# First attention of a two-layer block: probabilities transposed by DMA, and each item's work spread over six steps

## The chip, the cores and the metric

One NeuronCore of a Trainium2 chip. The metric is device time in microseconds (us) from start to end of the program: before the change 837.07 (median of 3 runs, 836.23 to 838.88).

## What is computed

A "macaron" block of two layers on 4 x 256 tokens of width 256: half a feed-forward net, attention, half a feed-forward net, twice, each behind a layer norm. The change is in the first attention (16 query heads and 4 key heads of 128, rotary embedding, softmax over a banded mask):

```
q = q * cos + _rotate_half(q) * sin
k = k * cos + _rotate_half(k) * sin
...
scores = jnp.einsum('bhqd,bhkd->bhqk', q, k) * scale
mask = iq >= ik - WIN
scores = jnp.where(mask[None, None, :, :], scores, -inf)
attn = jax.nn.softmax(scores, axis=-1)
out = jnp.einsum('bhqk,bhkd->bhqd', attn, v)
return out.transpose(0, 2, 1, 3).reshape(b, s, H * DH) @ Wo.T
```

The second layer's feed-forward net is a mixture of 8 experts, which routes rows of tokens through tables in DRAM (`xs_rows`, `yt_rows`).

## The kernel before, in words

Every product runs with operands split into two f16 parts, a high part (ScalarE copies it) and a low part (VectorE subtracts the high part), in three passes (`product`). The order of the work is written out by hand: each engine has its own list, and the lists meet only in semaphores.

The attention goes over two halves of the tokens (`hf`, two sequences of 256 each). In a half there are 32 items, one per head and sequence, and a step of `step0(hf, p, x)` starts one: `p` counts pairs of heads (8), `x` the four items of a pair. `x` 0 and 1 belong to one head, 2 and 3 to the next. The helper `lagged(p, x, k, n)` names the item started k steps ago. An item's life before the change:

- TensorE (L1672 to L1713): scores into a PSUM bank (step 0), four f32 transposes of the probabilities (L1695, two steps later), values times probabilities (three steps later), projection with Wo (four steps later).
- VectorE, DVE in the profile (L1252 to L1282): maximum of each row (L1258), shift (L1261), low half of the transposed probabilities (L1274), reciprocal of the sums (L1278), low half of the output (L1281).
- ScalarE, ACT in the profile (L744 to L772): high half of the transposed probabilities (L751), two exponentials (L757), high half of the output (L763).
- GpSimd, POOL in the profile (L597 to L609): scales the probabilities by the reciprocals (L607).

Between these stands the rope of the next heads, one head per two steps: TensorE's query product into bank `QB` (`queries`, at `x` 0 and 2), two ScalarE copies that swap halves (`rope_swapped`, L737, L738, at odd `x`), on VectorE the cosine product out of PSUM (`rope_cosine`, L1244, at even `x`), on GpSimd the sine product (`rope_sine`, L590, at odd `x`) and the sum (`rope_add`, L595, at even `x`), then the high half on ScalarE (`rope_high`, L742) and the low half on VectorE (`rope_low`, L1250). A query product waits until the cosine of the head before has read the one bank:

```
if x in ((1, 2) if isinstance(p, int) and p == 0 else (0, 2)) and ...:
    queries(hf, 2 * p + 2 + x // 2, QB, r + 2 + x // 2, r + 2 + x // 2)
```

The steps `p` = 1 to 6 are a loop on every engine. The items still in the pipe at the end of the first half are finished among the key, value and first query products of the second half, those of the second half in the first step of the feed-forward net that follows (`last_steps0`). The output is added to X on DVE (L1012).

SP issues the DMAs: all loads at the start, then twice a zero fill (L469) and a column of "free" marks (L471) for the two tables `xs_rows`, one per expert pass; it then has nothing to do until the attention's last projection.

Of the kernel before, what the change touches and what calls it, by code (L numbers as in the profile page):

```python
# [88 lines left out]
def macaron(nc, x_in, wa_in, wb_in, wc_in, wd_in, wg_in, rope0_in, rope1_in, mask_in, idf_in,  # L89
# [3 lines left out]
    with ctx:  # L93
# [46 lines left out]
        PR0 = ARENA[:, 0:1024].rearrange("p (a n) -> p a n", a=2)  # L140
        PT0 = ARENA[:, 1024:2048].bitcast(F16).rearrange("p (a s n) -> p a s n", a=2, s=2)
# [27 lines left out]
        IDP = sb("IDP", [P, ROWS // P + TT], I32)  # L169
        FREE = sb("FREE", [P, ROWS // P], F32)  # L170
# [19 lines left out]
        XS = [nc.dram_tensor(f"xs_rows{m}", [ROWS, ROW], F32, kind="Internal").ap() for m in range(2)]  # L190
# [20 lines left out]
        QB, OB = 4, 7  # L211
# [35 lines left out]
        pt_done, pt_hi, pt_lo = sem("pt_done"), sem("pt_hi"), sem("pt_lo")  # L247
# [167 lines left out]
        def lagged(i, x, k, n):  # L415

            if isinstance(i, int) and not 0 <= 4 * i + x - k < 4 * n:
                return None
            return (i - 1 if x < k else i), (x - k) % 4
# [27 lines left out]
        def _(sp):  # L447
# [19 lines left out]
            for table in XS:  # L467
                t3 = table.rearrange("(a p) d -> p a d", p=P)
                sp.dma_start(t3[:, :, 0:D + 1], ROUT[:, 0:D + 1].rearrange("p (o n) -> p o n", o=1)  # L469
                             .broadcast_to([P, ROWS // P, D + 1])).then_inc(dma_z, 16)  # L470
                sp.dma_start(t3[:, :, D + 1:ROW], FREE[:, :].rearrange("p (a o) -> p a o", o=1),  # L471
                             allow_slow_non_contiguous=True).then_inc(dma_z, 16)
            sp.wait_ge(proj_done, 2 * NS0)
# [6 lines left out]
            def expert_blocks(m):  # L480
# [3 lines left out]
                for b in range(NBK):  # L484
# [4 lines left out]
                    sp.dma_start(XB[:, g % 3, :], XS[m][ds(row * P, P), :]).then_inc(xb_in[g % 3], 16)  # L489
# [6 lines left out]
            expert_blocks(0)  # L496
            expert_blocks(1)
# [7 lines left out]
        def _(pool):  # L505
# [44 lines left out]
            def scatter(n, hf, tiles=range(TPH)):  # L550

                m = ROUTED.index((n, hf)) // 2
                pool.wait_ge(dma_z, 64)
                pool.wait_ge(idx_done, ROUTED.index((n, hf)) + 1)
                for t in (TPH * hf + i for i in tiles):
                    for k in range(2):
                        pl.indirect_dma_start(XS[m], bass.IndirectOffsetOnAxis(ap=IDX[:, k, t:t + 1], axis=0),  # L557
# [39 lines left out]
            def step0(hf, p, x):  # L597
                st, r = NS0 * hf + 4 * p + x, RU * hf + KV0 + 2 * p
                more, before = not (isinstance(p, int) and p == P0 - 1), not (isinstance(p, int) and p == 0)
# [4 lines left out]
                pool.wait_ge(recip_done, st + 1)  # L604
                pr = PR0[:, x % 2, :].rearrange("p (q k) -> p q k", q=2)
                rs = ST[:, x % 2, 3, :].rearrange("p (q k) -> p q k", k=1)
                pl.tensor_tensor(pr, pr, rs.broadcast_to([P, 2, S]), ALU.mult).then_inc(norm_done, 1)  # L607
# [42 lines left out]
            attention0(1, 2, 0)  # L650
            run_glu(pool, 1, 0, glu_step, glu_side)
# [28 lines left out]
        def _(act):  # L680
# [63 lines left out]
            def step0(hf, p, x):  # L744
                st, r = NS0 * hf + 4 * p + x, RU * hf + KV0 + 2 * p
                more, before = not (isinstance(p, int) and p >= P0 - 1), not (isinstance(p, int) and p in (0, P0))
                if lagged(p, x, 2, P0):
                    act.wait_ge(pt_done, st - 1)
                    after(act, pv_done, st - 3)
                    bank = odd_bank(hf) + 1 if x % 2 else 6  # L750
                    sc.activation(PT0[:, x % 2, 0, :], PS[:, bank, :], ACT.Copy, scale=SP).then_inc(pt_hi, 1)  # L751
                if lagged(p, x, 0, P0):

                    act.wait_ge(shift_done, st + 1)
                    bank = odd_bank(hf) if x % 2 else 5
# [18 lines left out]
            def attention0(hf, n, th):  # L774
# [16 lines left out]
                if hf:  # L791
                    value_high(0)
# [1246 lines left out]
```

## Time and profile before the change

| | |
|---|---|
| runs (3), median | 837.07 us |
| the profiled execution, own time | 835.15 us |
| its span, first to last instruction | 833.3 us |
| mean granted TensorE clock | 0.936 |
| busy over the span: PE, DVE, ACT, POOL | 86%, 75%, 55%, 48% |
| busy in the stretch 180 to 200 us (inside the attention): PE, DVE, ACT, POOL | 19.74, 15.81, 16.07, 13.62 of 20 us |
| first scores of the first half, of the second half | 110.5, 239.9 us |
| last projection of the attention | 351.8 us |

Busy time is the time in which an engine had an instruction under way. Matmuls are pipelined, so that the starts of two that follow each other are nearer together than the durations say: how fast TensorE streams is read from starts, how long an engine is held likewise. An idle time stands in brackets behind a row, with the engine and line that ended it. Times within the span are from its start.

### The profile page before, as it was taken

The numbers are of one execution on the slowest core, as the hardware profiler recorded it, in microseconds if no ns is written. First come the engines' busy times: TensorE is split into PE (matmuls) and PEld (weight loads), VectorE is DVE, ScalarE is ACT, GpSimd is POOL, SyncE is SP. The second block draws the span as 40 slices with busy tenths as digits, with TensorE's granted clock in tenths as the row PEclk, the third lists the DMA queues.
The fourth block names the chain that finished last, engine by engine and source line by source line (L and its number), as shares of the span: only waits on it lengthen the run. The fifth ranks groups of instructions, "written<-read, shape, count | busy, mean of one in ns | idle before, by whom it ended". The sixth has DMA issues, their size and how long they took to land. (4 is left out here: it accounts for less than half of the span.)

```text
span 833.3 us, 17601 instructions
## 1 busy us (share of the span) xinstructions
PE 712.8 (86%) x5515; PEld 481.6 (58%) x5515; DVE 627.9 (75%) x1436; ACT 458.0 (55%) x1033; POOL 402.5 (48%) x412
## 2 busy tenths in 40 slices
PE   7898969999969999989898699765698498978985
PEld 3555447777637777655555466433586397645652
DVE  5989878778787878699977677544897687676656
ACT  3444568878758888545423266325474476324551
POOL 4544766667667667358636177324004320331440
PEclk9999979999999999999999799966799598998998
DMA  9999995000000000030001233300000010012324
GB/s 375 327 300 185 226 231 2 0 0 0 2 0 1 0 0 0 6 116 1 1 14 58 77 114 110 129 1 1 1 1 2 7 46 2 1 52 84 116 84 164
DMA packets 64945, 59.07 MB, mean 71 GB/s; under 512 B 29106, under 2 KB 59186, under 8 KB 64370
## 3 DMA queue, kind: packets, MB, share of 16 engines
q1 hardware_dynamic: 60706, 47.85, 23.7%
q0 software_dynamic: 3744, 10.26, 3.5%
q8 instruction: 36, 0.59, 0.3%
q14 instruction: 27, 0.22, 0.1%
q10 hardware_dynamic: 432, 0.15, 0.1%
HBM read 27.92 MB, written 30.33 MB: 70 GB/s over the span
## 5 line engine op out<-in xcount | busy, mean ns | idle before, releaser
L1492 PE MATMUL PS<-XT,WA 128*128 128x512 f16 x432 | 100.4, 380 | 0.0
L607 POOL TENSOR_TENSOR ARENA<-ARENA,ST 128x512 f32<-128x512 f32 x64 | 66.6, 1040 | 64.0 <-DVE ST L1278 64.0
L724 ACT ACTIVATE ARENA<-T 128x512 f16<-128x512 f32 (+1 forms) x56 | 35.2, 628 | 109.9 <-DVE T L1156 102.4
L1492 PE MATMUL PS<-WA,ARENA 128*128 128x256 f16 (+2 forms) x960 | 68.6, 212 | 12.9 <-DVE ARENA L1165 11.9
L1492 PEld LDWEIGHTS PS<-WA,ARENA 128*128 128x128 f16 x960 | 56.6, 97 | 29.4 <-DVE ARENA L1165 18.0
L566 POOL DMA_INDIRECT yt_rows<-WA,DIX x46 | 45.4, 987 | 55.4 <-ACT WA L856 43.4
L1492 PEld LDWEIGHTS PS<-XT,WA 128*128 128x128 f16 (+1 forms) x432 | 42.3, 98 | 44.1 <-issue 0.8
L1492 PE MATMUL PS<-KVR,ARENA 128*128 (+1 forms) x384 | 57.9, 279 | 7.9 <-DVE ARENA L1250 4.6
L1258 DVE TENSOR_REDUCE ST<-PS 128x2 f32<-128x512 f32 x64 | 43.9, 686 | 26.1 <-PE PS L1492 25.3
L757 ACT ACTIVATE ARENA<-PS,ST 128x256 f32<-128x256 f32 x128 | 59.3, 470 | 7.0 <-DVE ST L1261 6.8
L1492 PE MATMUL PS<-XT,WC 128*128 128x512 f16 x264 | 60.6, 379 | 2.4 <-DVE T L1149 1.4
L595 POOL TENSOR_TENSOR T<-T 128x512 f32<-128x512 f32 x40 | 52.6, 1314 | 8.1 <-DVE T L1244 2.6
L590 POOL TENSOR_TENSOR T<-T,ROPE 128x512 f32<-128x512 f32 x40 | 50.9, 1272 | 10.4 <-ACT T L738 10.3
L1492 PE MATMUL PS<-ARENA,KVR 128*128 128x256 f16 x384 | 52.4, 272 | 2.6 <-DVE ARENA L1281 2.5
L1165 DVE TENSOR_TENSOR ARENA<-T,ARENA 128x512 f16<-128x512 f32 (+1 forms) x48 | 42.0, 876 | 16.5 <-ACT ARENA L724 15.9
L1492 PE MATMUL PS<-XT,WB 128*128 128x512 f16 x192 | 48.0, 388 | 5.7 <-DVE T L1244 4.2
L1492 PE MATMUL PS<-WB,ARENA 128*128 (+1 forms) x384 | 52.4, 273 | 0.3 <-DVE ARENA L1281 0.3
L1149 DVE SCALAR_TENSOR_TENSOR T<-T,PS 128x512 f32<-128x512 f32 (+1 forms) x56 | 38.0, 679 | 18.0 <-ACT T L716 17.6
L716 ACT ACTIVATE T<-PS 128x512 f32<-128x512 f32 (+1 forms) x56 | 33.1, 591 | 31.9 <-PE PS L1492 31.7
L1492 PE MATMUL PS<-WE,WA 128*128 x276 | 50.2, 319 | 0.0
L1492 PEld LDWEIGHTS PS<-KVR,ARENA 128*128 128x128 f16 x384 | 32.9, 99 | 26.6 <-issue 7.2
L557 POOL DMA_INDIRECT xs_rows<-XN,IDX x32 | 32.8, 1024 | 32.1 <-DVE IDX L1107 23.6
(184 smaller groups left out, 1803.0 us busy)
## 6 DMA issues: line engine op xcount, KB each, us to landing
xs_rows<-ROUT SPq DMA_DIRECT2D x2, 9252.0 KB, 46.1
WA<-xs_rows SPq DMA_DIRECT2D x46, 129.0 KB
WB<-wb_dram SPq DMA_DIRECT2D x1, 4096.0 KB, 21.4
WC<-wc_dram SPq DMA_DIRECT2D x1, 2304.0 KB, 26.5
WA<-wa_dram SPq DMA_DIRECT2D x4, 512.0 KB, 6.8
WA<-wa_dram SPq DMA_DIRECT2D x1, 2048.0 KB, 12.7
WA<-yt_rows SPq DMA_DIRECT2D x4, 512.0 KB, 4.1
WB<-yt_rows SPq DMA_DIRECT2D x4, 512.0 KB, 5.8
```

The costliest lines, as they stand in the source:

```text
L557: pl.indirect_dma_start(XS[m], bass.IndirectOffsetOnAxis(ap=IDX[:, k, t:t + 1], axis=0), XN[:, t // 2, t % 2, :], None, bounds_check=ROWS ...
L566: pl.indirect_dma_start(YT, bass.IndirectOffsetOnAxis(ap=DIX[:, b:b + 1], axis=0), YB[:, g % 3, :], None, bounds_check=2 * ROWS + 2 * TOK ...
L590: pl.tensor_tensor(t2, t2, ROPE0[:, 1:2, :].broadcast_to([P, 2, S]), ALU.mult).then_inc(rope_sin, 1)
L595: pl.tensor_tensor(T1[:, a, :], T1[:, a, :], T2[:, a, :], ALU.add).then_inc(rope_sum, 1)
L607: pl.tensor_tensor(pr, pr, rs.broadcast_to([P, 2, S]), ALU.mult).then_inc(norm_done, 1)
L716: sc.activation(T1[r, 0, :], PS[r, GATE[a], :], ACT.Tanh, scale=0.5 / (SX * SW)).then_inc(tanh_done, 1)
L724: sc.activation(HH[r, a, 0, :], T3[r, :], ACT.Copy).then_inc(hid_hi, 1)
L757: sc.activation(PR0[:, x % 2, qt * S:(qt + 1) * S], PS[:, bank, qt * S:(qt + 1) * S], ACT.Exp, bias=ST[:, x % 2, 1, qt:qt + 1], scale=SC0 ...
L1149: v.scalar_tensor_tensor(T2[r, 0, :], T1[r, 0, :], 1.0, PS[r, GATE[a], :], ALU.add, ALU.mult).then_inc(gated, 1)
L1165: v.tensor_tensor(HH[r, a, 1, :], T3[r, :], HH[r, a, 0, :], ALU.subtract).then_inc(hid_lo, 1)
L1258: v.tensor_reduce(ST[:, x % 2, 0, :], PS[:, bank, :].rearrange("p (q k) -> p q k", q=2), AX.X, ALU.max).then_inc(max_done, 1)
L1492: ins = te.matmul(dst, left(a), right(b), start=first and n == 0, stop=last and n == 2, skip_group_check=True)
```

## The change

The probabilities are no longer transposed by TensorE. ScalarE and VectorE split them, before transposing, into f16 halves side by side (`PH0`, four buffers), and SP issues one DMA per item that transposes the eight 128 x 128 blocks into `PT0` (four buffers); TensorE waits for its landing (`pt_in`). An item's work now spans six steps: exponentials one step behind the maximum, reciprocal and scaling two, halves of the probabilities three, values five, projection six. The low half of the probabilities now reads SBUF in both inputs. The freed PSUM banks hold a second query bank (`query_bank`) and a second output bank; a query product waits for the cosine one head further back. The two DRAM tables of rows become one, filled once; its column of marks is written again by SP between the two expert passes (`free_rows`), and waits on `dma_z` count accordingly.

```
-                if lagged(p, x, 2, P0):
-                    pe.wait_ge(norm_done, st - 1)
-                    after(pe, pt_lo, st - 3)
-                    bank = odd_bank(hf) + 1 if a else 6
-                    for qt in range(2):
-                        for kt in range(2):
-                            ins = te.transpose(PS[:, bank, kt * S + qt * P:kt * S + (qt + 1) * P],
-                                               PR0[:, a, qt * S + kt * P:qt * S + (kt + 1) * P], IDF[:, :])
-                    ins.then_inc(pt_done, 1)
-                if item := lagged(p, x, 3, P0):
+                if item := lagged(p, x, 5, P0):
                     pp, xx = item
                     g = pp // (GRP // 2)
-                    pe.wait_ge(pt_lo, st - 2)
-                    after(pe, ot_lo, st - 3)
+                    pe.wait_ge(pt_in[xx], turned_count(hf, pp))
+                    after(pe, ot_lo, st - 6)
...
-                    queries(hf, 2 * p + 2 + x // 2, QB, r + 2 + x // 2, r + 2 + x // 2)
+                    queries(hf, 2 * p + 2 + x // 2, query_bank(hf, x // 2), r + 2 + x // 2, r + 1 + x // 2)
```

SP:

```
+            def probabilities(hf, p, x):
+                it = NS0 * hf + 4 * p + x
+                sp.wait_ge(ph_lo, it + 1)
+                after(sp, pv_done, it - 3)
+                sp.dma_start(PT0[x].rearrange("p s (g n) -> p (s g) n", n=P), PH0[x].rearrange("p s n -> p (s n)"),
+                             transpose=True).then_inc(pt_in[x], 16)
...
             expert_blocks(0)
+            free_rows()
             expert_blocks(1)
```

ScalarE:

```
+                if item := lagged(p, x, 3, P0):
+                    pp, xx = item
+                    act.wait_ge(norm_done, st - 2)
+                    after(act, pt_in[xx], turned_count(hf, pp - 1))
+                    sc.activation(PH0[xx][:, 0, :], PR0[xx], ACT.Copy, scale=SP).then_inc(ph_hi, 1)
+                if item := lagged(p, x, 1, P0):
+                    xx = item[1]
+                    act.wait_ge(shift_done, st)
...
                 if x % 2 and more:
-                    rope_swapped(r + 2 + x // 2, QB, x // 2)
-
+                    rope_swapped(r + 2 + x // 2, query_bank(hf, x // 2), x // 2)
+                if item := lagged(p, x, 5, P0):
+                    a = item[1] % 2
+                    act.wait_ge(pv_done, st - 4)
+                    sc.activation(OT0[:, a, 0, :], PS[:, OB + a, 0:S], ACT.Copy, scale=1 / SP).then_inc(ot_hi, 1)
```

GpSimd, in the step (the order sum, scaling, sine stays) and between the key ropes of the second half:

```
-                pool.wait_ge(recip_done, st + 1)
...
+                if item := lagged(p, x, 2, P0):
+                    xx = item[1]
+                    pool.wait_ge(recip_done, st - 1)
...
                     rope_sine(RU * hf + i, i % 2)
                     rope_add(RU * hf + i, i % 2)
+                    if hf and i < 2:
+                        step0(0, P0, i)
```

VectorE: the step now begins with the reciprocal of the item two steps old, then the rope piece, then the low half of the item three steps old, then maximum and shift, and ends with the low half of the output:

```
+                if item := lagged(p, x, 3, P0):
+                    ph = PH0[item[1]]
+                    dve.wait_ge(ph_hi, st - 2)
+                    v.scalar_tensor_tensor(ph[:, 1, :], PR0[item[1]], SP, ph[:, 0, :], ALU.mult,
+                                           ALU.subtract).then_inc(ph_lo, 1)
```

What this does to the order on two engines. First ScalarE, inside the loop. Before, the step `x` = 1 from the high half of the transposed probabilities (L751) to the two rope copies (L737, L738):

```order
L751 ACTIVATE ARENA<-PS 128x512 [waits pv_done,pt_done]
L754 REGISTER_ALU
L757 ACTIVATE ARENA,ST<-PS,ST 128x256 [waits shift_done]
L757 ACTIVATE ARENA,ST<-PS,ST 128x256
L763 ACTIVATE ARENA<-PS 128x256 [waits pv_done]
L734 REGISTER_ALU
L263 REGISTER_ALU [waits rope_in]
L737 ACTIVATE T2<-PS 64x512 [waits rope_sum]
L738 ACTIVATE T2<-PS 64x512
```

Now, step `x` = 1 from the high half of the probabilities (L783) over the exponentials (L789) and the rope copies (L769, L770) to the high half of the output (L797):

```order
L783 ACTIVATE WB<-ROUT 128x512 [waits pt_in2,norm_done]
L786 REGISTER_ALU
L789 ACTIVATE ARENA,ST<-PS,ST 128x256 [waits shift_done]
L789 ACTIVATE ARENA,ST<-PS,ST 128x256
L766 REGISTER_ALU
L269 REGISTER_ALU [waits rope_in]
L769 ACTIVATE T2<-PS 64x512 [waits rope_sum]
L770 ACTIVATE T2<-PS 64x512
L796 REGISTER_ALU
L797 ACTIVATE ARENA<-PS 128x256 [waits pv_done]
```

The high half waits for GpSimd's scaling (`norm_done`) where it waited for TensorE's transposes (`pt_done`); the output's high half has moved from ahead of the rope copies to behind them.

Second VectorE, where an odd step of the loop ends and the even one after it begins. Before, from the low half of the output (L1281) over maximum (L1258), shift (L1261), cosine (L1244) and the low half of the transposed probabilities (L1274) to the reciprocal (L1278):

```order
L1281 SCALAR_TENSOR_TENSOR ARENA<-PS,ARENA 128x256 [waits ot_hi]
L1256 REGISTER_ALU
L1258 TENSOR_REDUCE ST<-PS 128x2 [waits scores]
L1261 TENSOR_SCALAR ST<-ST 128x2 [waits max_done]
L1242 ISA
L1244 TENSOR_TENSOR T1<-PS,ROPE0 128x512 [waits rope_lo,rope_swap]
L1274 SCALAR_TENSOR_TENSOR ARENA<-PS,ARENA 128x512 [waits pt_hi]
L1277 ISA
L1278 RECIPROCAL ST<-ST 128x2 [waits exp_done]
```

Now, from the low half of the output (L1318) over reciprocal (L1293), cosine (L1279), low half of the probabilities (L1305), maximum (L1310) to the shift (L1313):

```order
L1318 SCALAR_TENSOR_TENSOR ARENA<-PS,ARENA 128x256 [waits ot_hi]
L1292 ISA
L1293 RECIPROCAL ST<-ST 128x2 [waits exp_done]
L1277 ISA
L1279 TENSOR_TENSOR T1<-PS,ROPE0 128x512 [waits rope_lo,rope_swap]
L1305 SCALAR_TENSOR_TENSOR WB<-ROUT,WB 128x512 [waits ph_hi]
L1308 REGISTER_ALU
L1310 TENSOR_REDUCE ST<-PS 128x2 [waits scores]
L1313 TENSOR_SCALAR ST<-ST 128x2 [waits max_done]
L1318 SCALAR_TENSOR_TENSOR ARENA<-PS,ARENA 128x256 [waits ot_hi]
```

The cosine has come ahead of maximum and shift, right behind the low half of the output and the reciprocal; the low half of the probabilities reads ROUT (or ARENA) where it read PS.

## Rows read from the trace of the kernel before

**Rows 1.** PE's timeline, 193.5 to 202.8 us: start us, us, engine, line, operation, what ended an idle time.
```profile
193.91 0.49 PE L1492 MATMUL PS<-KVR,ARENA 128*128 x3
...
194.62 0.60 PE L1695 MATMUL PS<-IDF,ARENA 128*128 128x128 f32 x4
195.06 0.82 PE L1492 MATMUL PS<-ARENA,KVR 128*128 128x256 f16 x6
195.71 0.82 PE L1492 MATMUL PS<-WB,ARENA 128*128 x6
...
199.16 1.47 PE L1492 MATMUL PS<-XT,WB 128*128 128x512 f16 x6
200.47 0.49 PE L1492 MATMUL PS<-KVR,ARENA 128*128 x3
```

**Rows 2.** DVE's timeline, the same stretch.
```profile
194.82 0.69 DVE L1258 TENSOR_REDUCE ST<-PS 128x2 f32<-128x512 f32 x1 [1.04 <-PE PS L1492]
...
196.85 0.15 DVE L1278 RECIPROCAL ST<-ST 128x2 f32<-128x2 f32 x1
197.08 0.42 DVE L1281 SCALAR_TENSOR_TENSOR ARENA<-PS,ARENA 128x256 f16<-128x256 f32 x1
197.42 0.68 DVE L1258 TENSOR_REDUCE ST<-PS 128x2 f32<-128x512 f32 x1
...
198.31 0.69 DVE L1244 TENSOR_TENSOR T<-PS,ROPE 128x512 f32<-128x512 f32 x1
198.93 0.69 DVE L1274 SCALAR_TENSOR_TENSOR ARENA<-PS,ARENA 128x512 f16<-128x512 f32 x1
```

**Rows 3.** Timelines of POOL (first four rows) and ACT, 160 to 202.8 us.
```profile
161.03 1.04 POOL L607 TENSOR_TENSOR ARENA<-ARENA,ST 128x512 f32<-128x512 f32 x1
...
198.35 1.27 POOL L590 TENSOR_TENSOR T<-T,ROPE 128x512 f32<-128x512 f32 x1 [0.23 <-ACT T L738]
199.77 1.26 POOL L595 TENSOR_TENSOR T<-T 128x512 f32<-128x512 f32 x1
200.99 1.04 POOL L607 TENSOR_TENSOR ARENA<-ARENA,ST 128x512 f32<-128x512 f32 x1
...
197.07 0.60 ACT L737 ACTIVATE T<-PS 64x512 f32<-64x512 f32 x1
...
198.30 0.60 ACT L751 ACTIVATE ARENA<-PS 128x512 f16<-128x512 f32 x1
...
199.69 0.39 ACT L763 ACTIVATE ARENA<-PS 128x256 f16<-128x256 f32 x1
```

**Rows 4.** Timelines of POOL and DVE at two places, and line L974's durations (min/median/max).
```profile
220.30 1.27 POOL L590 TENSOR_TENSOR T<-T,ROPE 128x512 f32<-128x512 f32 x1 [0.36 <-ACT T L738]
221.72 1.52 POOL L595 TENSOR_TENSOR T<-T 128x512 f32<-128x512 f32 x1
...
220.91 1.21 DVE L1250 TENSOR_TENSOR KVR<-T,KVR 128x512 f16<-128x512 f32 x1
...
336.50 0.89 DVE L1261 TENSOR_SCALAR ST<-ST 128x2 f32<-128x2 f32 x1
...
L974 DVE SCALAR_TENSOR_TENSOR WA<-WA x8: 678/912/1578, 10.4 to 42.0; 128x512 f16<-128x512 f32 x8
```

**Rows 5.** DMA issues: line, engine, operation, count, KB each, median us to landing.
```profile
out_dram<-X SPq DMA_DIRECT2D x4, 256.0 KB, 2.2
...
xs_rows<-FREE SPq DMA_DIRECT2D x2, 36.0 KB, 48.6
```

**Rows 6.** Stretch 220 to 240: its length, busy us by engine, granted clock, DMA share, GB/s.
```profile
220.00:240.00 20.00, 15.04 (x84) 7.89 (x83) 17.62 (x32) 13.23 (x24) 15.20 (x14) 1.00 0.00 1
```

**Rows 7.** Timelines: SP and POOL late in the program, DVE between the halves.
```profile
533.56 0.97 SPq L493 DMA_DIRECT2D WB<-yt_rows  x2
...
664.53 1.08 POOL L557 DMA_INDIRECT xs_rows<-XN,IDX  x1 [10.83 <-DVE IDX L1107]
...
229.03 0.68 DVE L1012 SCALAR_TENSOR_TENSOR X<-PS,X 128x512 f32<-128x512 f32 x1
```

More of the change, by code:

```diff
@@ L598, in step0 @@
                 st, r = NS0 * hf + 4 * p + x, RU * hf + KV0 + 2 * p
-                more, before = not (isinstance(p, int) and p == P0 - 1), not (isinstance(p, int) and p == 0)
+                more, before = not (isinstance(p, int) and p >= P0 - 1), not (isinstance(p, int) and p in (0, P0))
                 if x == 0 and before:
@@ L650, in _ @@
             attention0(1, 2, 0)
+            for x in range(2):
+                step0(1, P0, x)
             run_glu(pool, 1, 0, glu_step, glu_side)
@@ L745, in step0 @@
                 st, r = NS0 * hf + 4 * p + x, RU * hf + KV0 + 2 * p
-                more, before = not (isinstance(p, int) and p >= P0 - 1), not (isinstance(p, int) and p in (0, P0))
-                if lagged(p, x, 2, P0):
[L748 to L755, printed above, removed]
-                    for qt in range(2):
-                        sc.activation(PR0[:, x % 2, qt * S:(qt + 1) * S], PS[:, bank, qt * S:(qt + 1) * S],
-                                      ACT.Exp, bias=ST[:, x % 2, 1, qt:qt + 1], scale=SC0 / SQ ** 2,
-                                      accum_out=ST[:, x % 2, 2, qt:qt + 1]).then_inc(exp_done, 1)
@@ L803, in attention0 @@
                     step0(hf, 0, x)
-                with act.Fori(1, P0 - 1) as p:
+                for x in range(4):
+                    step0(hf, 1, x)
+                with act.Fori(2, P0 - 1) as p:
                     for x in range(4):
@@ L948, in _ @@
             attention0(1, 2, 0)
-            for x in range(3):
+            for x in range(4):
                 step0(1, P0, x)
+            step0(1, P0 + 1, 0)
             act.wait_ge(dma_c, 16)
@@ L1253, in step0 @@
                 st, r = NS0 * hf + 4 * p + x, RU * hf + KV0 + 2 * p
-                more, before = not (isinstance(p, int) and p >= P0 - 1), not (isinstance(p, int) and p in (0, P0))
+                more, before = not (isinstance(p, int) and p >= P0 - 1), not (isinstance(p, int) and p in (0, P0, P0 + 1))
+                if item := lagged(p, x, 2, P0):
+                    a = item[1] % 2
+                    dve.wait_ge(exp_done, 2 * st - 2)
+                    v.reciprocal(ST[:, a, 3, :], ST[:, a, 2, :]).then_inc(recip_done, 1)
+                if x == 0 and before:
+                    rope_cosine(r + 1, query_bank(hf, 1), 1)
+                if x == 2 and more:
+                    rope_cosine(r + 2, query_bank(hf, 0), 0)
+                if x == 1 and before:
+                    rope_low(r + 1, 1, QT0[:, 1, 1, :], QT0[:, 1, 0, :])
+                if x == 3 and more:
+                    rope_low(r + 2, 0, QT0[:, 0, 1, :], QT0[:, 0, 0, :])
+                if item := lagged(p, x, 3, P0):
[3 more added lines that the diff above has]
+                                           ALU.subtract).then_inc(ph_lo, 1)
                 if lagged(p, x, 0, P0):
@@ L1320, in attention0 @@
                     step0(hf, 0, x)
-                with dve.Fori(1, P0 - 1) as p:
+                for x in range(4):
+                    step0(hf, 1, x)
+                with dve.Fori(2, P0 - 1) as p:
                     for x in range(4):
@@ L1465, in _ @@
             attention0(1, 2, 0)
-            for x in range(3):
+            for x in range(4):
                 step0(1, P0, x)
+            step0(1, P0 + 1, 0)
             glu(1, 0)
@@ L1745, in attention0 @@
                 queries(hf, 0, QB, r + KV0, r + KV0 - 1)
-                for i in range(0 if hf else KV0 - 1, TPH - 1):
+                if hf:
+                    step0(0, P0 + 1, 0)
+                    values(0)
+                    step0(0, P0 + 1, 1)
+                for i in range(1 if hf else KV0 - 1, TPH - 1):
                     values(i)
@@ L1758, in attention0 @@
                     step0(hf, 0, x)
-                with pe.Fori(1, P0 - 1) as p:
+                for x in range(4):
+                    step0(hf, 1, x)
+                with pe.Fori(2, P0 - 1) as p:
                     for x in range(4):
```

103 lines of the change are left out of this document (53 added, 50 removed).

## The prediction

> **What bounds the kernel now.** I read four views in turn. The table of stretches first: in the first attention TensorE looks full (19.7 of each 20 us in the table above), so removing its transposes seems to promise their time. The timeline of PE shows what they are. A step (one item's scores and the older items' work) streams scores in 0.71 us, four transposes in 0.44, probabilities times values in 0.65, the projection in 0.65, and every second step a query product of 1.31 [rows 1]. A pair of steps streams 2 x 2.45 + 1.31 = 6.21 us. The period of a pair, over six of them, is (200.99 - 161.03) / 6 = 6.66 us [rows 3]. So 0.45 us of a pair is not TensorE's.
>
> The timeline of DVE says whose it is. DVE idles once per pair, 1.04 us, until the scores behind a query are there, and then works without a gap: reduction, shift, low half of a head, low half of the probabilities, reciprocal, low half of the output, reduction, and at 198.31 the cosine of the next head [rows 2]. That cosine ends at 199.00 and the next query starts at 199.16 [rows 1, 2], because the query waits for the one bank that the cosine reads. Query, scores, seven DVE instructions, cosine, query: this ring has no slack, and it, not TensorE's stream, sets 6.66 us. The change opens it: queries get a second bank and wait for the cosine before. Without it and without transposes PE would need 2 x 2.01 + 1.31 = 5.33 us a pair. What is late next decides everything.
>
> **The ring that the change closes.** Take an odd step of ScalarE (the first order listing) and count from the start of its two rope copies, using today's durations.
> 1. The copies start at 0 and take 1.23 us; the copy of the output now stands behind them and takes 0.39 (198.30 - 197.07, and the row at 199.69) [rows 3]. Done: 1.62.
> 2. DVE (second order listing): the output's low half starts at 1.65, occupies DVE 0.34, the reciprocal 0.23, then the cosine starts at 2.22 [rows 2]. Its sum on POOL could start at 2.22 + 0.69 + 0.08 = 2.99; the sine alone would have let it start at 198.35 - 197.07 + 1.42 = 2.70 [rows 3].
> 3. But 0.62 after the cosine's start DVE issues the new low half of the probabilities, with both inputs in SBUF; the old one read PSUM. Such an instruction and POOL's exclude each other: DVE's subtraction at 220.91 took 1.21 us in place of 0.69, ending 0.55 after POOL's of 220.30 ended, and POOL's next took 1.52 in place of 1.26, ending 1.12 after DVE's [rows 3, 4]. The same form as the new one took 0.68 us at best and 1.58 at worst [rows 4]. Thus: low half 2.84 to 3.52, sum ends 3.52 + 1.12 = 4.64.
> 4. POOL now scales an item two steps old, in the next even step right behind this sum: it ends at about 4.64 + 1.04 = 5.68 (today 1.22 from start to start [rows 3]). I add 0.04 for the shift, which slips in between.
> 5. ScalarE's next odd step begins with the high half of just that item: start 5.76. High half and two exponentials hold it 199.69 - 198.30 = 1.39 today [rows 3]; I take 1.44, since the source is SBUF now, and the next rope copies start at 7.20.
>
> So a pair takes 7.20 us, 0.54 more than now, with PE idle for 1.9 us of it. Without the exclusion of step 3 the chain gives 6.75; without DVE's part as well (sum at 2.70) 6.46. Below that DVE stands: 6.66 less its 1.04 us of idle time is 5.6 us a pair [rows 2, 3]. There are 14 pairs with queries in each half of the tokens, so 28: **28 x 0.54 = +15.1 us**, bounds 28 x (6.46 - 6.66) = -5.6 and, if a second exclusion bites, the rival below.
>
> **Step by step, the rest.**
> - *64 x 4 transposes off PE*: 64 x 0.44 = 28.2 us of stream, worth nothing while the ring holds; in the last eight steps, which have no query, at best 2 x 6 x 0.44 = 5 us. I take nothing, since the shift then also meets POOL's scaling: the shift at 336.50 took 0.89 us, not 0.17, waiting for POOL's instruction [rows 4].
> - *64 DMA transposes of 256 KB on SP's queue*. No row shows one. Lower bound: 256 KB to DRAM landed in 2.2 us. Upper bound: the column of 9216 pieces landed in 48.6 us, 5.3 ns a piece; 1024 rows of 256 bytes would be 5.4 us [rows 5]. I take 3.5, nearer the first, since these are no 4-byte pieces. Between the low half (3.52) and the output's copy two ScalarE steps on, PE has 6 us for it, so both bounds hide as latency. As a rate, transfers must follow each other within 7.2 / 2 = 3.6 us; the upper bound breaks that (rival).
> - The Trainium skill, "DMA: Bandwidth & Descriptors", Latency and other measured facts, gives 261 GB/s for a DMA transpose, an estimate of 1.0 us here, and would leave the sum as it is; "VectorE: DVE Perf Modes", The three transpose paths, gives 1309 ns for one 128x128 block, and taken eight times would be 10.5 us an item. No run here shows either yet.
> - *Deeper pipe, between the halves*. On POOL the last two items' scalings move behind the first and the second rope of the next half. The second sum ends at 223.24 [rows 4]; with two scalings before it or behind, the last item is scaled at about 225.4, its halves take 0.60 + 0.68, the DMA 3.5, the product 0.65, the output's halves 0.9, the projection 0.65: 232.5. DVE adds that result to X at 229.03 today [rows 7]. **+4 us**, and 1 more for the exclusions: **+5**, bounds 1 (the DMA hides) and 9.
> - *At the end of the second half*: flush of six steps in place of four, DMA in place of transposes and a ScalarE copy: 3.5 - 1.0 less cover: **+2**, bounds 0 and 4.
> - *One DRAM table in place of two*: 9.25 MB less to fill, and its column written again between the expert passes. SP issues that behind the gathers at 533.56, and POOL's first scatter of the second pass stands at 664.53 [rows 7]; 48.6 us of landing hide in 131. Nothing. If SP were late, that scatter is what would wait. SP's queue is otherwise idle in the attention.
> - *TensorE's clock*: the stretch 220 to 240 shows 15.04 us busy of 20 at a granted 1.00 [rows 6], and the new loop is as busy (5.33 / 7.2 = 74%). No term.
>
> Sum: 15.1 + 5 + 2 = +22.1 us on the profiled execution's 835.15, so 857.3. The median of the runs is 1.9 above that execution, so I predict **859 us**.
>
> **Rivals.**
> - *Longer ring (slower still)*. Counting on, the shift of an odd step becomes ready 0.1 to 0.2 us before POOL starts the next sine. If it misses, it waits out the 1.27 us [rows 3], and the output's low half with it: the pair takes about 8.2 us, 28 x 1.0 more, 887 us. For it: the margin is smaller than my errors. Against: the rows, added, just miss it.
> - *The DMA rate becomes the bound*. Over 3.6 us per transfer, each 1 us costs 64 us; at 5.4 the kernel takes 859 + 64 x 1.8 = 974. Both the waits for the transfers on PE and SP would show it. Against: the 2.2 us for the same bytes.
> - *Faster: the ring does not close*. If the scaling on POOL ran ahead of the rope sum by an item, so that ScalarE's high half waits for nothing, DVE's and ScalarE's own work would set about 5.5 us a pair: 28 x (5.5 - 6.66) = -32, plus 7 for the flushes: about 812. It decides from the point where a pair falls below 6.5 us. Against: POOL's order is sine, sum, scaling, and ScalarE's wait counts exactly the scaling behind that sum.
> - *Sizes only*: the chain at 6.46, the flushes hidden: 835.
>
> **How the numbers follow.** Forecast 0.50; longer ring 0.20; DMA rate 0.12; faster 0.11; the no-change case 0.07. A measurement of this kernel tells about 0.3% (2.5 us) from no change. Slower: 0.50 + 0.20 + 0.12 = 0.82; same 0.07; faster 0.11. The range reaches down to 840 (the chain without the exclusion at 6.75 is 28 x 0.09 + 5 = +7, less 4 for flushes that hide) and up to 893 (the longer ring with the upper flush bound); left out are the faster case and most of the DMA case. The forecast's own range is 846 to 872.
>
> **What would show it.** Right: no transposes on PE and PE busy near 75%; between two rope copies of ScalarE 7.2 us; ScalarE's high half, now of the probabilities, waits for POOL's scaling; low halves on DVE of over 1 us beside POOL. Wrong: PE waiting for the DMA in each step, SP issuing without a pause, or pairs under 6.5 us with ScalarE or DVE full.

## The result, and the profile after

Four runs of the changed kernel have a median of 854.32 us (850.85 to 855.35), four of the kernel before 837.98 us (836.23 to 840.58). The ratio is 1.019, with a 95% interval of 1.016 to 1.023: 16 us slower. The prediction was 859 us, 840 to 893. The profiled execution took 855.31 us, its span 853.5 us at a mean granted clock of 0.932.

The page of the profile after: busy us and share by engine, and the DMA engines' busy tenths in 40 slices.

```profile
PE 691.6 (81%) x5259; PEld 454.7 (53%) x5259; DVE 651.7 (76%) x1436; ACT 460.1 (54%) x1033; POOL 426.1 (50%) x412
...
DMA  9999114333413334440001233290000010012324
```

PE is busy 691.6 us instead of 712.8, so the transposes did leave it, and the DMA slices 8 to 17, all 0 before, now show the transfers. Inside the attention the same stretch as in the table above (its length, then PE, PEld, DVE, ACT, POOL, the clock, the DMA share, GB/s):

```profile
180.00:200.00 20.00, 16.46 (x129) 11.79 (x129) 16.92 (x36) 14.65 (x41) 14.76 (x12) 1.00 0.40 76
```

PE fell from 19.74 to 16.46 us of 20, DVE and POOL rose from 15.81 to 16.92 and from 13.62 to 14.76. The clock stayed at 1.00. Now one pair of steps in full. ACT's timeline: the two rope copies (L769, L770) start a pair; L797 is the output's high half, L774 the rope's, L783 that of the probabilities, L789 an exponential.

```profile
179.74 0.59 ACT L769 ACTIVATE T<-PS 64x512 f32<-64x512 f32 x1
...
180.97 0.39 ACT L797 ACTIVATE ARENA<-PS 128x256 f16<-128x256 f32 x1
...
184.47 0.63 ACT L774 ACTIVATE ARENA<-T 128x512 f16<-128x512 f32 x1 [1.40 <-POOL T L621]
185.46 0.63 ACT L783 ACTIVATE WB<-ROUT 128x512 f16<-128x512 f32 x1 [0.37 <-POOL ROUT L635]
...
187.03 0.59 ACT L769 ACTIVATE T<-PS 64x512 f32<-64x512 f32 x1
```

From 179.74 to 187.03 is one pair, 7.29 us. ACT waits in it twice for POOL: 1.40 us for the rope sum, 0.37 for the scaling. Over nine pairs (136.64 to 201.44, same row) the period is 7.20 us, by turns 7.13 and 7.30; before it was 6.66. DVE and POOL in the same pair, the rows that answer to [rows 2] and [rows 3]:

```profile
181.39 0.42 DVE L1318 SCALAR_TENSOR_TENSOR ARENA<-PS,ARENA 128x256 f16<-128x256 f32 x1 [0.53 <-ACT ARENA L797]
...
182.02 0.69 DVE L1279 TENSOR_TENSOR T<-PS,ROPE 128x512 f32<-128x512 f32 x1
182.63 0.68 DVE L1305 SCALAR_TENSOR_TENSOR WA<-ARENA,WA 128x512 f16<-128x512 f32 x1
...
183.95 0.51 DVE L1313 TENSOR_SCALAR ST<-ST 128x2 f32<-128x2 f32 x1
```

```profile
181.03 1.27 POOL L616 TENSOR_TENSOR T<-T,ROPE 128x512 f32<-128x512 f32 x1 [1.52 <-ACT T L770]
182.79 1.64 POOL L621 TENSOR_TENSOR T<-T 128x512 f32<-128x512 f32 x1 [0.50 <-DVE T L1279]
184.40 2.48 POOL L635 TENSOR_TENSOR ROUT<-ROUT,ST 128x512 f32<-128x512 f32 x2
```

DVE: output's low half, cosine, low half of the probabilities (182.63), shift (183.95); reciprocal and maximum lie between. POOL: sine (L616), sum (L621), two scalings (L635). The sum takes 1.64 us, where it took 1.26 [rows 3]: it started 0.16 after DVE's low half and got under way behind it. The shift took 0.51 instead of 0.17 and ended with POOL's sum. Over the whole run L1305 has a mean of 1.02 us, where the low half that read PSUM had 0.69.

The transfers: landing, and PE's waits for them (us in total, times, longest).

```profile
ARENA<-WA SPq DMA_TRANSPOSE x32, 3.1
...
PE PS L1532 <- DMA WE<-WB: 2.1, 2, 1.9
...
PE PS L1532 <- DMA WC<-WB: 1.6, 4, 0.6
...
PE PS L1532 <- DMA ARENA<-WA: 1.2, 2, 0.7
```

They land in 3.1 us (median). PE waits for one eight times in the whole run, 4.9 us, and never in the rhythm of the loop: every wait is between the halves or in the last steps.

Where the difference of the two spans, 20.2 us, lies:

| stretch | before | after | difference |
|---|---|---|---|
| first half, first to last scores | 101.4 | 107.3 | +5.9 |
| last scores to first scores of the second half | 28.0 | 31.0 | +3.0 |
| second half, first to last scores | 100.8 | 106.1 | +5.4 |
| last scores to last projection | 11.1 | 13.9 | +2.7 |
| from there to POOL's scatter at 736.74 (before) and 753.82 (after) | | | 0.0 |
| from that scatter to the end | 96.6 | 99.7 | +3.1 |

The last row is no work of the change: in its stretch 817 to 837 the granted clock is 0.91, in the answering stretch of before 1.00. The traced runs of the experiments bear this out: from the same scatter to the end the kernel before takes 99.2 us in e1 and 99.7 in e9 (clock 0.91 there in both), the changed kernel 95.4 us in e3 (1.00). Another run of the changed kernel, at a mean clock of 0.944, has a span of 849.0. So the change itself costs 17.1 us, and the medians say 16.3.

### The profile page after: what moved, and what is told of

Same layout as the page of the kernel before. It is cut to its first block and busy times, and to the rows that moved or that the text cites. A ratio compares the mean times of both kernels' runs of the same rounds, so it can differ in the third digit from the quotient of the medians.

```text
span 853.5 us, 17074 instructions
## 1 busy us (share of the span) xinstructions
PE 691.6 (81%) x5259; PEld 454.7 (53%) x5259; DVE 651.7 (76%) x1436; ACT 460.1 (54%) x1033; POOL 426.1 (50%) x412
## 5 line engine op out<-in xcount | busy, mean ns | idle before, releaser
L616 POOL TENSOR_TENSOR T<-T,ROPE 128x512 f32<-128x512 f32 x40 | 51.7, 1293 | 54.9 <-ACT T L770 54.9
L621 POOL TENSOR_TENSOR T<-T 128x512 f32<-128x512 f32 x40 | 62.8, 1570 | 11.3 <-DVE T L1279 9.2
L1532 PEld LDWEIGHTS PS<-WB,ARENA 128*128 128x128 f16 x384 | 34.9, 98 | 29.5 <-issue 17.5
L1532 PE MATMUL PS<-XT,WB 128*128 128x512 f16 x192 | 50.0, 401 | 0.0
L1532 PE MATMUL PS<-WC,ARENA 128*128 128x256 f16 (+1 forms) x288 | 40.8, 298 | 9.2 <-DVE ARENA L1200 9.1
L925 ACT ACTIVATE ARENA<-PS,LNSP 128x768 f32<-128x768 f32 x32 | 28.9, 902 | 29.4 <-PE PS L1871 29.4
L1310 DVE TENSOR_REDUCE ST<-PS 128x2 f32<-128x512 f32 x64 | 43.6, 681 | 0.0
```

What stands on the lines that cost most here:

```text
L616: pl.tensor_tensor(t2, t2, ROPE0[:, 1:2, :].broadcast_to([P, 2, S]), ALU.mult).then_inc(rope_sin, 1)
L621: pl.tensor_tensor(T1[:, a, :], T1[:, a, :], T2[:, a, :], ALU.add).then_inc(rope_sum, 1)
L925: sc.activation(PR1[:, q % 2, :].rearrange("p (b n) -> p b n", b=2), PS[:, bank:bank + 2, 0:384], ACT.Exp, bias=LNSP[:, :], scale=SC1 / SQ ...
L1310: v.tensor_reduce(ST[:, x % 2, 0, :], PS[:, bank, :].rearrange("p (q k) -> p q k", q=2), AX.X, ALU.max).then_inc(max_done, 1)
L1532: ins = te.matmul(dst, left(a), right(b), start=first and n == 0, stop=last and n == 2, skip_group_check=True)
```

## The experiments

Each ratio is to runs of the kernel before on the same chip, with its 95% interval. "Pair" is the period between the rope copies on ScalarE, read from its timeline in mid-loop.

| run | edit | ratio | pair, us |
|---|---|---|---|
| (the change) | | 1.019 (1.016 to 1.023) | 7.13, 7.30 |
| e1 | before, 1 transpose of 4 | 1.000 (0.998 to 1.002) | 6.56, 6.77 |
| e2 | before, short low half | 0.999 (0.997 to 1.001) | 6.56, 6.77 |
| e3 | after, short low half | 1.007 (1.004 to 1.010) | 6.75, 6.91 |
| e4 | after, transfers twice | 1.023 (1.020 to 1.027) | 7.13, 7.30 |
| e5 | after, scaling before sum | 1.030 (1.026 to 1.034) | 7.35, 7.40 |
| e6 | after, rope's high half late | 1.035 (1.028 to 1.041) | 7.66, 7.80 |
| e7 | after, both | 1.009 (1.006 to 1.012) | 6.86 |
| e8 | after, both, copies first | 1.022 (1.017 to 1.027) | 7.08, 7.47 |
| e9 | before, query late | 0.989 (0.987 to 0.991) | 6.35, 6.40 |
| e10 | before, high half late | 1.119 (1.116 to 1.121) | 10.3, 10.5 |
| e11 | before, both | 1.050 (1.048 to 1.053) | 7.95, 8.16 |
| e12 | e9, 1 transpose of 4 | 0.993 (0.990 to 0.996) | 6.35, 6.40 |

**e1: do the transposes count?** Three of four are left out in the loop steps.

```
-                    for qt in range(2):
-                        for kt in range(2):
+                    whole = isinstance(p, int)
+                    for qt in range(0 if whole else 1, 2):
+                        for kt in range(0 if whole else 1, 2):
```

> The kernel before, with one of the four transposes of an item in the loop steps and the other three left out (their part of the probabilities is stale there). TensorE's stream falls by 3 x 0.11 = 0.33 us in each of 48 steps, 15.8 us in all. My theory: the ring of query, scores, VectorE and cosine bounds a pair at 6.66 us and the transposes lie in its shadow: 0 to -2 us, pairs of 6.6 to 6.66. Rival (TensorE's stream bounds): -14 to -16 us, pairs of 6.0.

837.93 against 838.03 us: nothing. A row of PE's timeline and three of ACT's (an exponential, L757, between two rope copies):

```profile
196.62 0.50 PE L1492 MATMUL PS<-KVR,ARENA 128*128 x3 [0.28 <-DVE ARENA L1250]
...
195.89 0.47 ACT L757 ACTIVATE ARENA<-PS,ST 128x256 f32<-128x256 f32 x1 [0.22 <-DVE ST L1261]
...
197.21 0.59 ACT L737 ACTIVATE T<-PS 64x512 f32<-64x512 f32 x1
...
203.77 0.60 ACT L737 ACTIVATE T<-PS 64x512 f32<-64x512 f32 x1
```

PE now idles (0.28 for the low half of a head, and at 197.79 0.18 for that of the output) where it streamed transposes. ScalarE's exponentials, which stand behind the high half of the transposed probabilities, now wait 0.22 us for VectorE's shift: the shift, not the transposes, lets them start. The pair keeps its 6.56 us, to the digit. So the prize that the change goes for was zero, as predicted.

**e2: is VectorE's queue the ring before?**

```
-    v.scalar_tensor_tensor(PT0[:, x % 2, 1, :], PS[:, bank, :], ...
+    n = 512 if isinstance(p, int) else 64
+    v.scalar_tensor_tensor(PT0[:, x % 2, 1, 0:n], PS[:, bank, 0:n], ...
```

> The kernel before, with the low half of the probabilities on VectorE cut from 512 to 64 columns in the loop steps (the rest is stale there). My theory: one of these stands in the ring between the scores and the cosine, so a pair loses up to 0.5 us until TensorE's stream of 6.21 us ends it: 24 pairs x 0.45 = -9 to -11 us, pairs of 6.2. Rival (TensorE's stream bounds already): under 2 us.

836.92 against 838.03 us, pairs unchanged: a miss. My ring for the kernel before was wrong. Its rows, DVE's between ACT's and PE's:

```profile
192.29 0.59 ACT L737 ACTIVATE T<-PS 64x512 f32<-64x512 f32 x1
...
193.74 0.69 DVE L1244 TENSOR_TENSOR T<-PS,ROPE 128x512 f32<-128x512 f32 x1
194.35 0.21 DVE L1275 SCALAR_TENSOR_TENSOR ARENA<-PS,ARENA 128x64 f16<-128x64 f32 x1
...
194.59 1.47 PE L1493 MATMUL PS<-XT,WB 128*128 128x512 f16 x6
```

The low half (194.35) is short and stands behind the cosine; the one in the other step of the pair is short too, and both only lengthen VectorE's idle time. What then lets the cosine start? In [rows 2, 3] the copies run from 197.07 to 198.28 and the cosine starts at 198.31, and VectorE's own queue ahead of it (output's low half, maximum, shift) ends within 0.03 us of the copies. Both branches start at one instruction, ScalarE's copy of the output at 196.66, so this turn doesn't tell them apart. The other turn of the kernel before does (ACT's second copy, DVE's shift and cosine):

```profile
190.92 0.59 ACT L738 ACTIVATE T<-PS 64x512 f32<-64x512 f32 x1
...
191.53 0.17 DVE L1261 TENSOR_SCALAR ST<-ST 128x2 f32<-128x2 f32 x1
191.75 0.69 DVE L1244 TENSOR_TENSOR T<-PS,ROPE 128x512 f32<-128x512 f32 x1
```

The copies end at 191.51 and the cosine starts at 191.75, behind the shift: here VectorE's maximum and shift, which had to wait for their scores, release it. The cosine comes 1.45 us after the start of the copies (190.30), in the turn of [rows 3] 1.24, and this 0.21 is the difference of the two turns, 6.77 and 6.56 us. So the low half of the probabilities was wrong in my ring, and ScalarE was missing.

Behind the cosine the ring runs on through ScalarE. The rows of the kernel before that close it:

```profile
201.38 0.69 DVE L1258 TENSOR_REDUCE ST<-PS 128x2 f32<-128x512 f32 x1 [0.84 <-PE PS L1492]
202.10 0.17 DVE L1261 TENSOR_SCALAR ST<-ST 128x2 f32<-128x2 f32 x1
...
201.12 0.63 ACT L742 ACTIVATE ARENA<-T 128x512 f16<-128x512 f32 x1 [1.04 <-POOL T L595]
...
202.31 0.47 ACT L757 ACTIVATE ARENA<-PS,ST 128x256 f32<-128x256 f32 x1
...
203.62 0.60 ACT L737 ACTIVATE T<-PS 64x512 f32<-64x512 f32 x1
```

Copies 197.07, cosine 198.31, query 199.16, scores behind it 200.47 [rows 1], maximum 201.38, shift 202.10, exponentials 202.31, output copy 203.22, copies 203.62: 6.55 us. A second ring runs beside it: copies, sine 198.35, sum 199.77, rope's high half 201.12, high half of the probabilities 201.81, the same exponentials. This one has no query and no scores in it. In the kernel before it doesn't bound by itself: the step from 201.12 to 201.81 takes 0.69 us because the high half of the probabilities waits for the transposes (PE 201.18 to 201.78); in e9 the same step takes 0.54.

The total of e2 hides a loss. In its trace one early pair of each half takes 8.14 and 7.88 us instead of 6.45 and 6.46, where the granted clock is 0.50 (120 to 122 and 250 to 252; before 1.00). Of these 3.1 us, 2.7 are made up behind the attention, where nothing was changed.

**e3: does the exclusion cost what the prediction says?** The same cut in the changed kernel, where both inputs are in SBUF.

> The changed kernel, with the low half of the probabilities on VectorE cut from 512 to 64 columns in the loop steps of pairs 2 to 6 (the rest is stale there). My theory: its exclusion with GpSimd's rope sum is 0.45 us of the ring: the sum falls from 1.64 to about 1.3 us and starts no later, pairs go from 7.20 to 6.75 us; 20 pairs x 0.45 = -9 us on the changed kernel's 854, so 845. Rival (the exclusion is beside the path; ScalarE's order behind GpSimd's scaling, or the DMA, sets the pair by itself): under 3 us.

843.49 us, 10.8 less than the changed kernel's median. ACT, DVE and POOL:

```profile
183.60 0.59 ACT L769 ACTIVATE T<-PS 64x512 f32<-64x512 f32 x1
...
190.35 0.59 ACT L769 ACTIVATE T<-PS 64x512 f32<-64x512 f32 x1
...
186.25 0.22 DVE L1306 SCALAR_TENSOR_TENSOR WB<-ROUT,WB 128x64 f16<-128x64 f32 x1
...
186.41 1.26 POOL L621 TENSOR_TENSOR T<-T 128x512 f32<-128x512 f32 x1 [0.26 <-DVE T L1279]
```

The pair is 6.75 us from copies to copies (6.91 in the other turn), the sum back at 1.26. The prediction's chain without the exclusion gave 6.75. The cut makes VectorE's own work shorter too, but the sum waits for the cosine alone (0.26), and the pair fell by 0.38 and 0.39 us, just what the sum lost (1.64 to 1.26): it is the exclusion. It doesn't explain all of the 10.8 us. From the first to the last rope copies of the attention the traces differ by 7.6 us (244.2 and 236.6), which is 20 x 0.38; behind the scatter of the last pass, where nothing was cut, they differ by another 4.3 (99.7 and 95.4).

**e4: is the DMA rate or latency on the path?** Each transpose is followed by a second one of the same size into memory that nobody reads.

```
+                after(sp, dumped, 16 * it)
+                sp.dma_start(DUMP..., PH0[x]..., transpose=True).then_inc(dumped, 16)
```

> The changed kernel, with every DMA transpose followed on the same queue by a second one of the same size into memory that nobody reads, so twice the transfers and bytes. My theory: the transfers' rate and latency are not on the path (each lands in 3.1 us, TensorE has about 6 us for it): 0 to +3 us, and pairs still of 7.2 us. Rival (the DMA rate bounds or is close to it; two transfers of 3.1 us in a step of 3.6): pairs of 12.4 us or, if they overlap by half, over 8 us, +25 us and more.

859.3 us, 5 more than the changed kernel's 854.3 (the ratios, whose intervals overlap, say 4; 0 to 3 were expected), and pairs of 7.13 and 7.30 as before. Landing, and PE's waits:

```profile
WE<-WB SPq DMA_TRANSPOSE x16, 3.3
...
PE PS L1537 <- DMA ARENA<-WA: 4.7, 4, 2.1
...
PE PS L1537 <- DMA WC<-WB: 4.1, 4, 1.7
PE PS L1537 <- DMA WE<-WB: 3.7, 2, 2.0
```

The waits come to 12.5 us where they were 4.9, all between the halves and at the end. In the loop twice the transfers cost nothing.

**e5 to e8: can the new ring be opened?** e5 exchanges two instructions on GpSimd (scaling ahead of the rope sum). e6 moves the rope's high half on ScalarE behind the odd step's exponentials and its low half on VectorE with it. e7 does both; e8 puts the high half behind the rope copies instead, and the low half last in VectorE's step.

```
GpSimd, even steps (e5, e7, e8):  sum, scaling          ->  scaling, sum
ScalarE, odd steps (e6, e7):      exponentials, copies  ->  exponentials, rope_high, copies
VectorE, odd steps (e6, e7):      rope_low ahead of ph_lo  ->  behind the shift
```

> The changed kernel, with GpSimd's scaling of the probabilities ahead of the rope sum in even steps (the prediction's faster rival). My theory now: ScalarE's next step then waits for no scaling, but the sum ends a scaling later (4.9 to 5.5 us after the rope copies' start) and ScalarE's rope high half, which waits for the sum, stands ahead of the next step's work: 0.63 for it, 0.5 for the high half of the probabilities, 1.05 for two exponentials, so 7.1 to 7.75 us a pair, -3 to +15 us on the changed kernel's 854. Rival (the prediction's: ScalarE's wait for the scaling is the whole of it): pairs of 5.5 to 6 us, 812 to 825.

> The changed kernel, with ScalarE's high half of the rope sum moved from the end of an even step to behind the exponentials of the odd one, and VectorE's low half of it behind that step's shift; GpSimd's order as in the change. My theory: the wait for the scaling (5.7 us after the rope copies' start) still stands ahead of the exponentials, and the moved high half adds 0.6 behind them: 7.2 to 7.8 us a pair, 0 to +17 us. Rival (the rope sum itself bounds): pairs of 6.5 or less, under 838.

> The changed kernel with both of these: scaling ahead of the rope sum on GpSimd, and the rope's high half behind the exponentials. My theory: neither wait then stands ahead of the exponentials, and the ring that is left runs rope copies, sine, scaling, sum (ends at 4.9 to 5.5), high half, copies: 5.7 to 6.2 us a pair, 28 x (6.0 - 7.2) = -34 us: 815 to 830, below the kernel before. Rival (VectorE, 5.6 us of work a pair and its waits for GpSimd's port, or PE's waits for the transfers bound first): pairs of 6.6 to 7, 838 to 848.

> As the one with both moves, but the rope's high half stands behind ScalarE's rope copies and output copy of the odd step, and its low half last in VectorE's odd step. My theory: the sum is out of ScalarE's ring altogether, but the scores of the next step and VectorE's next step start only behind the low half (3.0 us after the copies' start): 6.3 to 6.7 us a pair, 829 to 840. Rival (only ScalarE's order counts): 5.6 us a pair, 810 to 815.

863.97, 868.13, 846.87 and 856.0 us. e5 and e6 fell where the chains put them: each takes away one of ScalarE's two waits for GpSimd (1.40 us for the sum, 0.37 for the scaling) and lengthens the other, to 1.93 for the sum in e5 and to 2.40 for the scaling in e6. The prediction's faster rival (pairs under 6.5 once the scaling leads) is refuted by e5. e7, with both, gains 1.0% over the change (the ratios 1.009 and 1.019), but 6.86 us a pair is not 6.0; its rival was right. e8 (7.08 and 7.47, where 6.3 to 6.7 were expected) missed in part for the same reason: its shifts wait for POOL too, and in every second pair one waits out the sine (188.22, 1.27 us instead of 0.17). That is what the prediction's longer ring was to suffer. DVE, POOL and ACT of e7 (L789 is an exponential):

```profile
185.84 1.45 DVE L1301 SCALAR_TENSOR_TENSOR WB<-ROUT,WB 128x512 f16<-128x512 f32 x1
...
187.92 0.52 DVE L1309 TENSOR_SCALAR ST<-ST 128x2 f32<-128x2 f32 x1
...
185.70 1.04 POOL L631 TENSOR_TENSOR ARENA<-ARENA,ST 128x512 f32<-128x512 f32 x1
186.70 1.72 POOL L621 TENSOR_TENSOR T<-T 128x512 f32<-128x512 f32 x1
...
188.48 0.48 ACT L789 ACTIVATE ROUT<-PS,ST 128x256 f32<-128x256 f32 x1 [0.99 <-DVE ST L1309]
```

The low half of the probabilities (L1301) waits for POOL's scaling (1.45 instead of 0.67), the shift (L1309) for POOL's sum (0.52 instead of 0.17), and the exponentials at 188.48 for the shift. The wait that ScalarE no longer has for the sum, it has through VectorE's wait for the same instruction.

**e9 to e12: the kernel before, with what e2 taught.** e9 moves the query product on TensorE from the end of the even step into the odd one, so that the scores no longer queue behind it:

```
+                if x % 2 and not (isinstance(p, int) and p >= P0 - 1):
+                    queries(hf, 2 * p + 2 + x // 2, QB, r + 2 + x // 2, r + 2 + x // 2)
                 if item := lagged(p, x, 3, P0):
...
-                if x in ((1, 2) if isinstance(p, int) and p == 0 else (0, 2)) and not (isinstance(p, int) and p >= P0 - 1):
-                    queries(hf, 2 * p + 2 + x // 2, QB, r + 2 + x // 2, r + 2 + x // 2)
```

> The kernel before, with one edit on TensorE: the query product moves from the end of an even step into the odd one, behind its scores and transposes. My theory after two misses: the ring that bounds the kernel before at 6.66 us a pair runs rope copies (ScalarE), cosine, query, scores behind it on TensorE's queue, reduction, shift, two exponentials, output copy, rope copies; this edit takes the query out from ahead of the scores, and what is left is the ring rope copies, sine, sum, rope high half, high half of the probabilities, exponentials, output copy, 6.45 to 6.55 us: -3 to -6 us. Rival (VectorE's queue between scores and cosine, as the prediction said): no change or, with the query up to 2 us later, slower.

> The kernel before, with the rope's high half moved on ScalarE from the end of an even step to behind the exponentials of the odd one, and its low half on VectorE behind that step's reciprocal. My theory: this opens only the second ring (sine, sum, high half); the one through the query stays at 6.56 and 6.77 us in turn and gets the 0.6 us of the high half between exponentials and copies: 0 to +17 us. Rival (sum and high half bound): faster by 3 us or more.

> The kernel before with both moves. My theory: both rings are open, ScalarE no longer waits for the rope sum, and TensorE's stream of 6.21 us a pair is the next bound: pairs of 6.2 to 6.35 us, 28 x (6.3 - 6.66) = -10 us, 825 to 830, faster than both kernels; the transposes would then be worth their time. Rival (the low half of a head, now late on VectorE, holds up the next even scores): pairs of 6.6 or more, no gain.

e9: 836.36 against 844.16 us on its chip, 1.1% faster than the kernel before, and so faster than both. The pairs, 6.35 and 6.40, are even below what I gave the second ring. ACT, POOL, and the stretch 180 to 200:

```profile
188.34 0.60 ACT L737 ACTIVATE T<-PS 64x512 f32<-64x512 f32 x1
...
192.34 0.63 ACT L742 ACTIVATE ARENA<-T 128x512 f16<-128x512 f32 x1 [0.98 <-POOL T L595]
...
194.69 0.59 ACT L737 ACTIVATE T<-PS 64x512 f32<-64x512 f32 x1
...
191.04 1.27 POOL L595 TENSOR_TENSOR T<-T 128x512 f32<-128x512 f32 x1
...
180.00:200.00 20.00, 19.96 (x167) 16.00 (x165) 18.61 (x38) 16.70 (x48) 14.31 (x13) 1.00 0.00 0
```

ACT works without a pause from 192.34 to the copies at 194.69, and what releases 192.34 is the sum. 28 pairs x (6.66 - 6.37) is 8.1 us; 7.8 were measured. Here too two waits all but coincide: the shift, held up by POOL's scaling (192.45, 0.88 us instead of 0.17), ends at 193.33, and the exponentials start at 193.37.

e10 and e11 are far slower than I expected (945.03 and 888.13 us), and the rival named for e11 came true. In e10:

```profile
188.09 1.31 DVE L1249 TENSOR_TENSOR ARENA<-T,ARENA 128x512 f16<-128x512 f32 x1 [0.35 <-ACT ARENA L742]
...
187.82 1.04 POOL L607 TENSOR_TENSOR ARENA<-ARENA,ST 128x512 f32<-128x512 f32 x1 [3.57 <-DVE ST L1273]
...
189.70 0.55 PE L1491 MATMUL PS<-KVR,ARENA 128*128 x3 [2.39 <-DVE ARENA L1249]
```

The low half of a head, moved late on DVE, meets POOL's scaling, takes 1.31 instead of 0.69 us, and the even scores (PE, 189.70) wait 2.39 us for it; in e11 1.72 us. In e10 the granted clock is low besides, 0.83 in the stretch 180 to 200 where e11 has 1.00; what of its 101 us is the clock's wasn't tried apart. I take it that the move pays only if that low half isn't late; no run shows it, and e11 couldn't show TensorE's 6.21 us.

**e12: with the query's ring open, do the transposes count at last?**

> The kernel before with the query behind the odd scores, and besides with one transpose of the four in the loop steps (three left out, as in the first experiment). My theory: its pairs of 6.35 and 6.40 us are the ring rope copies, sine, sum, rope high half, high half of the probabilities, exponentials, output copy, with no slack on ScalarE; the transposes are not in it: pairs within 0.03 us of these, 0.989 of the kernel before. Rival (with the ring of the query open, TensorE's stream of 6.21 us is what holds a pair at 6.37): pairs of 6.2 or less, 0.984 or less.

838.41 against 844.46 us. PE, and ACT's rope copies:

```profile
189.78 0.52 PE L1492 MATMUL PS<-KVR,ARENA 128*128 x3 [0.40 <-ACT ARENA L757]
...
190.29 0.59 ACT L737 ACTIVATE T<-PS 64x512 f32<-64x512 f32 x1
...
196.64 0.59 ACT L737 ACTIVATE T<-PS 64x512 f32<-64x512 f32 x1
```

PE idles 0.40 us ahead of the scores and 0.27 at 191.06, and in mid-loop the pairs stay at 6.35 and 6.40. The ratio is 0.993 and not 0.989, though the two intervals just overlap. In the trace most of these 3 us is in two pairs of each half, the second and third of the loop: 7.11 and 6.94, and 7.12 and 6.95, where e9 has 6.35 and 6.39, and 6.36 and 6.39. That is 2.6 us. In that place the granted clock of e12 is 0.57 (126 to 130) and 0.60 (252 to 256), that of e9 1.00. So it isn't the rhythm that loses them; that the clock does is my reading of the trace, and no run sets it apart. At any rate nothing is gained.

## Why the prediction was right, and where it was not

- *The transposes are worth nothing*: right, shown by e1, and by e12 even with one ring less.
- *What bounds the kernel before*: the number (6.66 us a pair, a ring through the single query bank) was right, the members were not. The step that failed is the sentence "Query, scores, seven DVE instructions, cosine, query". VectorE's maximum and shift are in it, and then ScalarE's exponentials, output copy and rope copies. The low half of the probabilities is beside it (e2). The next maximum and shift release the cosine in every second pair (191.75) and tie with the rope copies in the others; the other low halves and the reciprocal weren't cut one by one. e9 shows that the query ahead of the scores is in the ring. The step "the change opens it" held, but the ring of ScalarE and GpSimd right behind (6.37 in e9) was missed: even a change that only opened the query's ring had 0.3 us a pair to win.
- *The ring that the change closes*: right in each step that could be read. Copies to output copy 1.23 (predicted 1.23), cosine at 2.28 (2.22), low half at 2.89 (2.84), sum ends at 4.69 (4.64), scaling awaited at 5.72 (5.76), copies at 7.29 (7.20). Part of the last agreement is luck: from the scaling to the copies it is 1.57 us in both turns, where I took 1.44, and the scaling comes at 5.56 in the other turn; in the mean the two errors cancel. The price of the exclusion, 0.45, was 0.38 (e3). The sign "PE busy near 75%" came out as 82% (16.46 of 20 us): the 5.33 us of stream are counted from starts, busy time from durations.
- *The term 28 x 0.54 = 15.1* was 11.3 us (5.9 + 5.4). The difference per pair was right in mid-loop, the count was not: in the first half 12 periods carry it (122.77 to 208.58 after, 123.70 to 203.62 before: +5.9), the steps ahead of the first are 1.1 us shorter and those behind the last 1.1 longer.
- *Between the halves +5*: +3.0. *At the end +2*: +2.7. The DMA took 3.1 us (3.5 taken).
- *DMA*: at twice the rate still not bounding (e4). The landing of 3.1 us lies within the prediction's bounds from rows (2.2 to 5.4) and agrees with neither of the two estimates named behind them, 1.0 and 10.5 us. *One table*: its column was written again at 551.73 and the first scatter that needs it came at 681.22. Nothing, as costed; it wasn't tried apart.
- *TensorE's clock*: no term in the attention, right as to the cost, though the clock isn't 1.00 everywhere: in the first pairs of the loop it falls to 0.50 (124 to 126, and 260 to 262), where before it was 1.00. The pairs there are 6.82 and 7.05 us, the same as in the second half of e3, whose clock is 1.00 there. 3.1 us in the profiled run are from the clock in the last expert pass, a place of which I had said nothing.
- *The rivals*: the longer ring of 8.2 didn't come, though the shift does lose 0.34 us to POOL's sum (183.95): it isn't on the path there, since the exponentials that need it start at 186.00, behind the scaling. In e8 such a wait, of 1.27 us, does come. The faster rival was refuted as a mechanism by e5.

For the profiled execution the sum gave 857.3 us, and it took 855.3. That is closer than the terms deserve: those of the attention were 5.1 us too high (22.1 against 17.0), and 3.1 us of clock in the last pass, which no term foresaw, made up for most of it. That part is luck.

## What to carry to other kernels

An engine that is busy 99% of a stretch need not bound it: leave out part of its work in an experiment, and if its idle time grows by just that, the bound is a ring through other engines' queues. When a wait ends within a few hundredths of two candidates, the trace doesn't say which of them holds; follow each candidate round to where it started, and cut one. And work that moves from a PSUM source to SBUF sources on VectorE should be counted against GpSimd's time too, since the two then run one after the other.

## What the runs showed of the hardware that I had not expected

- The exclusion reaches very small instructions, but not all. A 128x2 multiplication from SBUF to SBUF on VectorE (the shift) took 0.51 us beside POOL's sum and 0.17 without it, and 0.89 in the kernel before at 336.50 [rows 4]; a 64-column low half took 0.83 us beside a scaling and 0.22 alone (e3). The reductions, cosines and output halves, which read PSUM, kept 0.68, 0.69 and 0.42 us throughout. So did the reciprocal, 128x2 from SBUF to SBUF like the shift: 0.15 to 0.17 us in all 64, and 0.15 at 189.02 in the middle of POOL's sine (188.31, 1.27 us). The Trainium skill, SBUF — State Buffer, Who interferes with whom, calls this an exclusive lock of a port pair that VectorE and GpSimd share, held for a whole instruction; the traces agree for the instructions that were hit: whichever comes second ends nearly its own duration after the first one's end (1.12 us for the sum of 1.26, 0.55 for e7's low half of 0.67, 0.02 for its shift of 0.17).
- In one such meeting both lose: at 182.63 VectorE came first and POOL's sum took 1.64 us; the shift that queued behind it then waited for the sum. A 0.68 us instruction put between two of POOL's so delayed both engines by turns.
- A DMA transpose of 8 blocks of 128x128 lands in 3.1 us, and with twice as many of them in 3.1 to 3.3 (e4).
